# Tiles of keys with a diagonal block alternate with tiles without one, from the second half batch on

## What is computed

```python
q, k, v = x @ Wq, x @ Wk, x @ Wv
latent_kv = (k + v) @ W_down_kv
k_rec, v_rec = latent_kv @ W_up_k, latent_kv @ W_up_v        # 16 heads of 8 each
scores = clip(einsum('bhqd,bhkd->bhqk', q, k_rec) * scale)
decay = exp(-0.0001 * abs(idx[:, None] - idx[None, :]))       # by the distance of query and key
attn = softmax(clip(scores * decay))
x = layernorm(x + (attn @ v_rec) @ Wo)
x = layernorm(x + moe(x) + shared(x))
```

## Time and profile before

| | us |
|---|---|
| median of 3 runs | 702.51 (697.26 to 703.01) |
| the profiled execution | 703.71 |
| its span, first to last instruction | 701.9 |

### The profile page before, as it was taken

The page is one execution under the profiler, slowest core; times in us unless marked ns, Lnnn a source line. Parts: engine busy times, 40 slices in busy tenths (PEclk is TensorE's granted clock), DMA queues, the critical chain, the costliest instruction groups (busy, mean ns, idle before and its releaser), DMA issues.

```text
span 701.9 us, 12880 instructions
## 1 busy us (share of the span) xinstructions
PE 657.5 (94%) x4763; PEld 293.2 (42%) x4763; DVE 311.5 (44%) x998; ACT 548.2 (78%) x640; POOL 274.6 (39%) x259
## 2 busy tenths in 40 slices
PE   7886999998999999999999999999999998899982
PEld 3321333332333333333333333333334987775641
DVE  3551423453344344734433453345343352275783
ACT  3765899997999999999999999999998433342342
POOL 1719354430460146046005634512552105637611
PEclk9998999998999999999999999999999999899997
DMA  5527995544256335525633586323446688642111
GB/s 160 163 79 269 379 386 194 195 147 141 91 196 226 109 130 200 192 91 196 196 102 114 209 279 186 106 83 94 148 147 199 185 261 264 203 124 76 38 54 49
DMA packets 73540, 116.83 MB, mean 166 GB/s; under 512 B 6592, under 2 KB 49152, under 8 KB 73472
## 3 DMA queue, kind: packets, MB, share of 16 engines
q1 hardware_dynamic: 54944, 102.06, 43.4%
q10 hardware_dynamic: 15456, 7.59, 3.7%
q0 software_dynamic: 3072, 6.30, 3.0%
HBM read 68.73 MB, written 48.76 MB: 167 GB/s over the span
## 4 chain that ended last, share of the span: by engine, by line
PE 73%; DMA 6%; DVE 5%; ACT 5%; SPq 4%; issue 3%; POOL 3%; ACTq 0%; POOLq 0%; DVEq 0%
PE ps L957 29%; PE ps L941 19%; PE ps L1088 6%; ACT probs L800 4%; PE ps L880 4%; DMA queries<-stack_dram 3%; PE ps L1083 3%; SPq L465 2%; SPq L475 2%; PE ps L1008 1%; DMA stack_dram<-stage 1%; PE ps L976 1%; PE ps L1097 1%; PE ps L1005 1%; PE ps L1101 1%
## 5 line engine op out<-in xcount | busy, mean ns | idle before, releaser
L800 ACT ACTIVATE probs<-ps 128x1024 f32<-128x1024 f32 x512 | 480.3, 1045 | 38.6 <-DVE ps L1413 30.6
L957 PE MATMUL ps<-probs,V 128*18 128x512 f32 x2048 | 273.5, 607 | 0.6 <-ACT probs L800 0.4
L941 PE MATMUL ps<-queries,keys 32*128 32x512 f32 (+3 forms) x1408 | 182.1, 413 | 14.3 <-DMA queries<-stack_dram 10.8
L1413 DVE TENSOR_TENSOR ps<-ps,cpk 128x256 f32<-128x256 f32 x256 | 101.8, 429 | 140.2 <-PE ps L941 126.8
L941 PEld LDWEIGHTS ps<-queries,keys 32*128 32x128 f32 x1408 | 92.4, 185 | 160.4 <-ACT probs L800 90.1
L593 POOL TENSOR_TENSOR stage<-qk,rows_sb 128x512 fp32r<-128x512 f32 x32 | 40.8, 1276 | 137.5 <-DVE qk L1260 132.0
L635 POOL DMA_INDIRECT sorted_dram<-xn,slots x48 | 47.1, 982 | 62.4 <-ACT probs L800 48.4
L846 ACT ACTIVATE probs<-ps 128x512 f32<-128x512 f32 x48 | 28.5, 597 | 54.3 <-PE ps L1088 23.8
L1088 PE MATMUL ps<-xnT,stage 128*128 128x512 f32 x128 | 58.9, 593 | 0.0
L957 PEld LDWEIGHTS ps<-probs,V 128*18 128x18 f32 x2048 | 34.6, 96 | 56.6 <-issue 40.9
L1535 DVE TENSOR_TENSOR probs<-probs,ps 128x512 f32<-128x512 f32 x48 | 32.7, 687 | 51.1 <-ACT probs L846 21.5
(11 more groups left out here) (192 smaller groups left out, 594.4 us busy)
## 6 DMA issues: line engine op xcount, KB each, us to landing
stack_dram<-stage SPq DMA_DIRECT2D x60, 512.0 KB, 6.5
keys<-stack_dram SPq DMA_DIRECT2D x30, 512.0 KB
queries<-stack_dram SPq DMA_DIRECT2D x30, 512.0 KB
keys<-stack_dram SPq DMA_DIRECT2D x30, 256.0 KB
keys<-expert_dram SPq DMA_DIRECT2D x28, 192.0 KB
sorted_dram<-y_pre SPq DMA_DIRECT2D x1, 4096.0 KB, 18.3
rows_sb<-expert_dram SPq DMA_DIRECT2D x16, 192.0 KB
V<-expert_dram SPq DMA_DIRECT2D x16, 192.0 KB
```

Of the source, the lines that this page charges most:

```text
L800: nc.scalar.activation(probs[:, m % 3, 2 * j:2 * j + 2, :], ps[:, 2 * s:2 * s + 2, :], ACT.Exp, scale=SCALE).then_inc(exp_done, 1)
L941: last = mm(bank[2 * s + i][:, lo:hi], keys[rows, u, kt // CT, v, tok(kt % CT)], queries[rows, u, v, lo:hi], start=True, stop=True)
L957: last = mm(bank[OUT_BANK][32 * i:32 * i + 2 * (HD + 1), :], V[:, c // 2 % 2, kt, k + i, half * (HD + 1):(half + 2) * (HD + 1)], probs[:, ...
L1413: tt(d, d, diag_fix.unsqueeze(1).to_broadcast([P, 2, P]), ALU.mult).then_inc(diag_done, 1)
```

## The change

`key_tile(m)` takes the place of `m % NT`. In half batch 0 it is the same. In the others it takes keys of the two halves in turn: for c even the near tiles 0, 1, 2, 3 at the even places and the far tiles 4 to 7 at the odd ones; for c odd the near tiles 4 to 7 at the even places and the far ones 0 to 3 at the odd ones. In both, a tile with a diagonal stands at each even place and one without at each odd place. The places of side work, the order of scores, outputs and side work on PE, and the order of diagonals and side results on DVE are as before. The marks for the first and last matmul of a sum go by the tile's number now and not by `kt`.

```diff
+        def key_tile(m):
+
+            c, i = m // TPC, m % NT
+            return i if c == 0 else i // 2 + CT * ((i + c) % 2)
+
         crossings = [0]
         for n in range(2 * TILES):
-            c, kt = n // 2 // TPC, n // 2 % NT
+            c, kt = n // 2 // TPC, key_tile(n // 2)
             crossings.append(crossings[-1] + crossing(c, kt))
@@ exponential
-                if crossing(m // TPC, m % NT):
+                if crossing(m // TPC, key_tile(m)):
@@ scores
-                Q, c, kt = m // NT, m // TPC, m % NT
+                Q, c, kt = m // NT, m // TPC, key_tile(m)
@@ outputs
-                Q, c, kt = m // NT, m // TPC, m % NT
+                Q, c, kt = m // NT, m // TPC, key_tile(m)
-                if kt == 0 and half == 0 and Q:
+                if m % (2 * NT) == 0 and Q:
-                              start=(kt == 0 and half == 0), stop=(kt == NT - 1 and half == 1))
+                              start=m % (2 * NT) == 0, stop=m % (2 * NT) == 2 * NT - 1)
@@ fix_diagonal
-                c, kt = m // TPC, m % NT
+                c, kt = m // TPC, key_tile(m)
```

## The result

The changed kernel has a median of 717.12 us (714.02 to 719.13, 6 runs), the kernel before one of 701.36 (697.26 to 703.01, 6 runs): ratio 1.0232, interval 1.0200 to 1.0264. A second comparison on another chip gave 714.04 against 699.35, ratio 1.0209 (1.0179 to 1.0239). That is +15.8 and +14.7 us; forecast were 717 and, as the sum, +14.7.

The account below looks back on a forecast made before the run. ACT was taken as the bound, at 1.87 us a tile; 8.8 + 7.3 + 1.5 - 2.9 = +14.7 us on the profiled 703.7 gave 718.4, and 717 us since that execution was 1.2 above its median; range 706 to 722.

Parts of the forecast that it names:

- the rule: ACT's attention tiles: side work is forgiven 0.22 us if the tile two places later has a diagonal, 0.68 if none.
- part 2: DVE, half batches 1 to 5: side results queue behind diagonals, so PE waits 0.5 us at 19 pairs: +7.3 us.
- Parts 1 and 2: Half batches 1 to 7: diagonals two places behind side work, +8.8 us; side results behind diagonals on DVE, +7.3.
- Part 3: Start of half batch 7: tile 2's diagonals stand behind the six order_blocks steps on DVE, delaying ACT: +1.5 us.
- Part 4: Starts of half batches 2, 4 and 6: ACT's earlier losses come out of PE's waits for loads: -2.9 us.
- What would show it: Signs in half batches 1 to 7: ACT idle about 33 us for 17.4, DVE waits well over 20 for 11.8.
- Less waiting: Rival, chance 0.20: PE's waits for side copies behind diagonals hardly count; 712 us, 711 against the median.
- No change: Rival, chance 0.16: in the attention, three slots and tiles without a diagonal take up small delays; +5, 708 us.
- Faster: Rival, chance 0.08: blocks of four diagonals hurt, so alternating cuts ACT's 11.8 us wait for DVE; 695 us.
- Dearer: Rival, chance 0.12: delays add up, half batches 2, 4 and 6 start 1 to 2 us later each; 722 to 725.

Follow-up runs that it names:

- run 5: Kernel before (natural order of keys) without the diagonal multiplications on DVE, ACT waiting for scores alone: 677.59 us, ratio 0.9834 to the kernel before.
- run 6: Changed kernel (alternating order) without the diagonal multiplications on DVE: 677.20 us, ratio 0.9830 to the kernel before.
- run 2: Against the changed kernel, no alternation: diagonals in blocks of four, but in the other half of each eight places: 720.62 us, ratio 1.0290 to the kernel before.
- run 11: Changed kernel with diagonals at the odd places instead of the even ones, executed again on another chip: 710.28 us, ratio 1.0170 to the kernel before.
- run 8: The kernel before once more, nothing changed, for the spread between executions: 689.57 us, ratio 1.0006.
- run 1: Changed kernel with diagonals at the odd places instead of the even ones, first execution: 714.93 us, ratio 1.0198 to the kernel before.
- run 7: Kernel before with diagonals placed by a table for the smallest idle time the prediction's formula gives: 691.92 us, ratio 1.0025 to the kernel before.
- run 9: The changed kernel itself again, on another chip: 714.04 us, ratio 1.0209 to the kernel before.
- run 3: Changed kernel with order_blocks called one tile later: 716.64 us, ratio 1.0212 to the kernel before.
- run 4: Changed kernel with DVE's copies of side results put ahead of the next tile's diagonals at 19 close pairs: 713.21 us, ratio 1.0174 to the kernel before.
- run 10: Changed kernel with side copies ahead of diagonals at the close pairs, executed again on another chip: 710.10 us, ratio 1.0152 to the kernel before.

## Why the prediction was right

**The bound and the rule.** ACT stayed the bound, and the rule's 0.22 us of side work forgiven ahead of a tile with a diagonal held in the new order. Half batches 1 to 6 have 24.7 us of idle time where it gave 25.2, and single tiles of half batch 5 agree: 0.42 at tile 2, 0.27 at 8, 0.37 at 10, 0.60 at 11, 0.64 at 18, 0.37 at 24, 0.55 at 26, where the prediction named 0.37, 0.27, 0.15 (0.39 with the wait of part 2), 0.69, 0.65, 0.37 and 0.5.

**Parts 1 and 2, +16.1 together.** Their sum of 27.3 holds, 27.9 in the trace without tile 2 of half batch 7. The cause was shown from three sides: without diagonals the orders are equal (runs 5, 6), with diagonals behind even more pieces it is worse (run 2), behind the odd ones better (run 11). No run tests the division into 8.8 and 7.3 apart, but the idle time fits only with both: half batches 1 to 6 have 24.7 us, for 17.9 by the rule without part 2 and 25.2 with it. All 19 waits came, of 0.48 on average instead of 0.5 to 0.55. The copy does not pass the diagonal though its data are ready, nor in 19 places here. The rule of the Trainium skill (PSUM — Partial Sum Buffer, "Engine vs sequencer instructions"), that VectorE's queue is strictly first in, first out, agrees with these 19 waits.

**Part 3, +1.5.** It is 1.44 us. Timeline of the changed kernel, start of half batch 7:

```profile
488.53 0.97 PE L946 MATMUL ps<-queries,keys 32*128 32x128 f32 x8
488.74 0.69 DVE L1422 COPY osb<-ps 128x512 f32<-128x512 f32 x1 [1.08 <-PE ps L962]
...
490.51 0.18 DVE L1368 SCALAR_TENSOR_TENSOR small<-small 128x24 f32<-128x24 f32 x1
490.73 0.76 DVE L1418 TENSOR_TENSOR ps<-ps,cpk 128x256 f32<-128x256 f32 x2
...
491.25 1.02 ACT L805 ACTIVATE probs<-ps 128x1024 f32<-128x1024 f32 x1 [1.44 <-DVE ps L1418]
```

The scores of the tile are ready from about 489 on; DVE comes to them at 490.73, and the exponential 0.52 later.

**Part 4, -2.9: the term that was mis-sized.** The waits at 4 and 6 went as forecast. That at 2 was to shrink to 1 to 2 us and is gone. PE's timeline there:

```profile
163.65 0.64 PE L946 MATMUL ps<-queries,keys 32*128 32x512 f32 x4
164.21 1.05 PE L962 MATMUL ps<-probs,V 128*18 128x512 f32 x8
165.20 1.09 PE L946 MATMUL ps<-queries,keys 32*128 32x512 f32 x4
```

The scores of half batch 2 start at 163.65 with 0.09 us of idle time, where before PE waited 3.17 us, to 163.55. The load's issue moved as worked out, from 155.37 to 156.87, by 1.5 for 1.4. What the step missed is twofold. First, it took the time of the load as fixed. From the issue of the first load to the first scores it was 8.2 us in that execution, at most 6.8 in the changed kernel and 6.5 in run 8, where PE waited only 1.45 us and ACT 0.93 at this tile. So first tiles gave back 4.0 us of ACT's idle time instead of 2.9. Second, it counted the wait alone and not what comes behind it: the prediction noticed that most of the old idle time over the rule lies in the few tiles behind the longest wait, and put nothing in the sum for its going. That was the low clock from 163.2 to 170.0 (the four matmuls of the first scores take 0.80 us in the earlier trace rows, for 0.51 elsewhere). Its going gave back another 1.4. The same is seen elsewhere: in runs 1 and 5 to 8 PE waited 1.45 to 2.42 us at this place, and the clock fell to 0.50 during the wait or within 1.8 us of its end and stayed there for some tiles (in run 8 tiles 2 and 3 lost 2.6 us). It does not follow each time: in runs 2 and 11 PE waited 1.34 and 1.96 us and the clock stayed at full.

**What nearly cancels this.** In half batch 7, tile 16 waits 1.18 us for the rule's 0.37: its diagonals begin at 518.97, 0.8 after its scores should have been ready (last section). In all, ACT's idle time rose by 11.9 us where the sum had 14.7: 1.1 and 1.4 less by part 4, while tile 16 and the small misses of the rule nearly cancel. The profiled executions differ by 12.1. The medians differ by 15.8, since the profiled execution of before was 2.3 above its final median and that of the changed kernel 1.3 below. That the median of 717.12 meets the 717 so closely is therefore partly luck: the sum of ACT's idle times accounts for 11.9 to 13.4 (from 16.5 of run 8 to 29.9 of run 9), and the last 1 to 4 us lie within what single executions differ by and have no row.

**A sign that did not agree with the sum.** "What would show it" named about 33 us of idle time. The sum on top of the trace gives 17.4 + 14.7 = 32.1; the rule alone, 27.3 + 1.5, gives 28.8, and the trace has 29.3. The difference is the old idle time over the rule, which the sum carried along although most of it belonged to a wait that the change shortens.

**The rivals.** *Less waiting* fell with the 19 waits of PE and with the tiles that pay for them, such as 10 and 11 of half batch 5 (0.37 and 0.60 us; 0.15 and 0.37 without the waits). *No change* fell because a lone diagonal behind side work does cost its full price: the tiles without a diagonal between them don't take it up. *Faster* fell with the result: diagonals in blocks cost 8.5 us in all (runs 8 and 5), so there was no such sum to win, and blocks on other places are the slowest of all (run 2). *Dearer* had the right observation, the load chain of the even half batches starts 1.5 us later, but its waits at the starts had more room than that.

## What to carry to other kernels

When one engine is the bound and others feed it in a fixed order, list for each of its steps how late its feeder may be, with and without an extra hop (here 0.68 and 0.22 us), and keep the steps with the extra hop away from places behind extra work; spreading them evenly puts more of them there. Where two short steps meet on an engine that takes its steps in order, turning them round gives back only a part (2.0 of the 11.9 us of added idle time here), so look for a place where they don't meet. A rule that is right tile by tile still needs the long rare steps and the waits for loads: where a gain ends in a wait for a load, it is given back. And look at the granted clock of every stretch before reading an idle time as the price of an order: behind a wait of PE the clock can be low, and then the tiles that follow are late as well.

## What was not expected of the hardware

**The expert part depends on the chip.** The same kernel has a median of 700.42, 689.38 and 699.35 us on the three chips. In the first profile of the kernel before the attention ends at 537.0 us and in run 8 (chip 2) at 535.6; the expert part takes 165.0 us in the one and 152.1 in the other (162.1 to 165.4 in runs 1 to 4, 152.1 to 152.5 in 5 to 8, 161.1 to 162.5 in 9 to 11). One stretch of it, the first profile and then run 8:

```profile
560.00:600.00 40.00, 35.76 (x264) 31.48 (x263) 13.61 (x47) 14.25 (x25) 11.16 (x12) 0.96 0.88 270
```

```profile
560.00:600.00 40.00, 39.66 (x289) 33.76 (x288) 17.10 (x52) 16.06 (x28) 13.84 (x14) 1.00 0.92 293
```

In the first the transfers moved 270 GB/s, on chip 2 293, and PE got less done (264 matmuls for 289). The granted clock differs too, 0.96 for 1.00 here and 0.95 for 0.97 over the expert part. Whether the transfers, the clock or something else is the cause was not tested. It bears on ratios only by the smaller total.

**TensorE's clock can make one profile mislead.** The same kernel had 33.5 and 26.2 us of idle time on ACT in two executions; half batch 7 lost 7.2 us for 2.4, 4.0 of the difference of 4.8 behind the fall of the clock to 0.50, and half batch 2 8.1 for 5.7. At full clock PE is not the bound in the attention; at 0.50 it is, with 1.91 us for a tile's outputs and 0.8 for its scores where ACT needs 1.87.

**A late signal that stays open.** At places 15 and 16 of half batch 7 a step that follows PE starts late: by 0.5 to 0.9 us in the changed kernel and in runs 2 to 4 and 9 to 11, by 1.6 in run 1, and a little in the first profile of the kernel before (there the second diagonal of tile 15, nearly hidden). It is in none of the four runs of chip 2 (5 to 8), with diagonals or without: run 8 has the kernel before, its exponential 0.60 us behind the scores. So it goes with the chip or its transfers rather than with the diagonals. In the changed kernel it is the diagonal, in run 11 an exponential:

```profile
518.06 1.05 PE L962 MATMUL ps<-probs,V 128*18 128x512 f32 x8
518.97 0.76 DVE L1418 TENSOR_TENSOR ps<-ps,cpk 128x256 f32<-128x256 f32 x2 [4.21 <-PE ps L946]
```

```profile
513.79 0.50 PE L946 MATMUL ps<-queries,keys 32*128 32x512 f32 x4
...
515.24 1.02 ACT L805 ACTIVATE probs<-ps 128x1024 f32<-128x1024 f32 x1 [0.75 <-PE ps L946]
```

PE's clock is at full there, and the ends of matmuls are modelled, so PE itself may be what is late. Transfers take up 0.5 to 1.0 of the DMA engines in the microsecond before and after; no run separates the two.
